# Counts of a graph kernel: a third of each row widened from SBUF by GpSimd and by a transfer, three row buffers, a lag of three

## The chip, the core and the metric

One NeuronCore of a Trainium2 chip runs the whole program in one launch. The metric is the device time of that launch in microseconds. The kernel before takes 4137.85 us (median of three runs, 4137.58 to 4137.88).

## The reference, cut to what matters

Four graph networks run one after the other on 6250 nodes of 128 features and 100000 edges. Each of their layers gathers the state of every edge's source node and adds it up at the edge's target node:

```python
for i in range(3):                                   # first network
    agg = segment_sum(h[src], dst, num_segments=6250)
    h = h + agg
    h = relu(bn(h @ W1[i] + b1[i]))
    h = relu(bn(h @ W2[i] + b2[i]))
# then: an attention layer with a GRU cell, five GRU steps over the same edges,
# and a last layer: segment_sum(h[src], dst) @ W.T + b
```

Between the networks stand a layer norm and additions. The input x is normalised row by row before the first layer, so that the first layer sums the normalised x over the edges.

## The kernel before, in words

Nodes are padded to 49 blocks of 128. The kernel never gathers by edge. It sorts the edges once, and from the sorted list it makes a matrix of counts: how many edges run from node s to node t, one byte each, 6272 rows of 6400 bytes, kept in HBM as `count`. Each layer's sum over the edges is then a product of the states with this matrix on TensorE: a block of 128 rows of bytes is read into SBUF (`ring`), widened to fp32r (`wide`), and multiplied with the states of the 128 source nodes. The states are cut in two parts, `hi` and `lo`, so that two matmuls with fp32r operands give the precision wanted. The target columns are handled in three thirds (`THIRDS`, `THIRD_PAIRS`), since PSUM holds no more than a third's sums at once.

The program has three stretches: `sort_edges` (to about 290 us), `fill_counts` (to 555 us) and then the layers, run by `Flow`, to the end. The change is in `fill_counts` alone, apart from one list of semaphores in `program` (line 2763).

**What the fill does.** For each of the 49 source blocks k it makes the 128 rows of the count matrix and stores them; beside that it already forms the sums of the middle third (`EARLY` = 1, 2048 columns) for the first layer, so that `Flow` is given that third (`given=(EARLY,)`). The engines run these programs, each written out by hand for all k and tied by semaphores:

- VectorE (L571 to 604), for each k: `apart` (an XOR of two int16 tables of 3200 columns, L579), `left` (a comparison of bf16 tables of 3200 columns, L580), `right` (a tensor_scalar on `apart`, L582), then `high` of block k - 2 (128 columns, L589) and `lo` of block k - `EARLY_LAG` (L596). It may run one block ahead of TensorE: before `apart` of block k it waits for all the matmuls of block k - 2. All inputs and outputs of these five lie in SBUF. After the last block it adds the finished sums to the state in four pieces of 512 columns (L602).
- TensorE (L607 to 639), for each k in four groups g: up to eight matmuls of 128 columns, one for each pair of column blocks, 25 in all (L621, `ps<-right,left`); with the last group a transpose of the state (L626); and behind each group two matmuls of 512 columns for the sums of block j = k - `EARLY_LAG`, with `hi` and with `lo` of block j (L634). The first of these waits for `hi`, `lo` and for the widened counts of block j.
- ScalarE (L641 to 676), for each k: the normalised state (L659), then for each group the move of the counts from PSUM to the row buffer as uint16, which is two count bytes (L667: three of 1024 columns and one of 128), with `hi` of a block (L654) behind the first and a spread of codes (L647) behind the second, and at last the transposed state (L674). Before it writes row buffer k % 2 it waits until the transfer of row k - 2 to HBM has landed.
- SyncE (L689 to 692): stores row k to `count` when its four groups are out.
- GpSimd (L678 to 686): waits until the store of row k has landed and until the slot of `wide` (four slots) is free, and then issues a transfer that reads the 2048 bytes of the middle third back from `count` in HBM and widens them to fp32r on the way into `wide` (L685). In this stretch it does nothing else.

The two row buffers lie in `net.aggT`, before and behind the columns of the middle third, which stay free until the sums are added. The stage ends when every engine is through its program; for GpSimd that means that the last store has landed.

The lines that the steps below touch most:

```python
        rows = [net.aggT[:, c0:c0 + ROW // 4].bitcast(U16) for c0 in (0, early.stop)]
        ...
                if k >= 2:
                    e.wait_ge(stored[k % 2], 16 * (k // 2))
        ...
                e.wait_ge(stored[k % 2], 16 * (k // 2 + 1))
        ...
                e.dma_start(wide[:, k % EARLY_SLOTS, :], count[k * P:(k + 1) * P, t0 * PAIR:t0 * PAIR + width])\
                    .then_inc(s[f"loaded{k % EARLY_SLOTS}"], 16)
```

Of the kernel before, what the change touches and what calls it, by code (L numbers as in the profile page):

```python
# [11 lines left out]
U8 = mybir.dt.uint8  # L12
U16 = mybir.dt.uint16
# [11 lines left out]
P = 128  # L25
NB = -(-N // P)
NP = NB * P
# [14 lines left out]
PAIR = 2 * P  # L42
NCHUNK = (NB + 1) // 2
ROW = NCHUNK * PAIR
# [13 lines left out]
THIRD_PAIRS = [(0, 10), (10, 8), (18, 7)]  # L58
# [20 lines left out]
GATE_SLOTS = 11  # L79
EARLY = 1  # L80
EARLY_BANK = 4
EARLY_LAG = 4
EARLY_CUT = 2
EARLY_SLOTS = 4
CODE_SLOTS = 4
# [443 lines left out]
def fill_counts(nc, net, count, hot, seen, stored):  # L529
# [4 lines left out]
    ps = net.ps  # L534
# [3 lines left out]
    PER = 8  # L538
    groups = -(-NCHUNK // PER)
    pieces = SUMS[EARLY]  # L540
    width = sum(size for _, size in pieces)
    codes_each = NCHUNK * RUN
    assert len(pieces) == groups == 4
    names = ["left", "apart", "right", "mm", "out", "spread", "normal", "turned", "state", "high", "hi", "lo", "summed", "whole",
             *[f"loaded{j}" for j in range(EARLY_SLOTS)]]
    with ExitStack() as tmp, stage(nc, *names, held=stored) as (block, s):
        left = [scratch(nc, tmp, f"left{u}", [P, P, NCHUNK], BF16) for u in (0, 1)]
# [4 lines left out]
        hi = scratch(nc, tmp, "hi", [P, CUT_SLOTS, P], F32R)  # L552
        lo = scratch(nc, tmp, "lo", [P, CUT_SLOTS, P], F32R)
        early = slice(THIRDS[EARLY][0] * P, sum(THIRDS[EARLY]) * P)
        rows = [net.aggT[:, c0:c0 + ROW // 4].bitcast(U16) for c0 in (0, early.stop)]
        codes_by = net.aggT[:, ROW // 4:ROW // 4 + CODE_SLOTS * codes_each // 2].bitcast(I16)
        assert early.start >= ROW // 4 + CODE_SLOTS * codes_each // 2 and early.stop + ROW // 4 <= NP and early.stop - early.start == width

        def of_block(table, k, run):
            row = table[:, k * NCHUNK * run:(k + 1) * NCHUNK * run]  # L560
# [8 lines left out]
        @block.vector  # L569
        def _(e):  # L570
            for k in range(NB + EARLY_LAG):  # L571
                u = k % 2
                if k < NB:
                    if k >= 2:
                        e.wait_ge(s["mm"], groups * (k - 1))
                    e.wait_ge(s["spread"], k + 1)
                    if k:
                        e.wait_ge(s["right"], k)
                    e.tensor_tensor(apart[:, :, :], marks_by[:, :, :], of_block(codes_by, k % CODE_SLOTS, RUN), ALU.bitwise_xor).then_inc(s["apart"], 1)  # L579
                    e.tensor_tensor(left[u][:, :, :], orders_by[:, :, :], of_block(row_of, k, 1), ALU.is_equal).then_inc(s["left"], 1)  # L580
                    e.wait_ge(s["apart"], k + 1)
                    e.tensor_scalar(flat(right[u]), apart[:, :, :], 256.0, 256.0, ALU.min, ALU.subtract).then_inc(s["right"], 1)  # L582
                j = k - EARLY_CUT
                if 0 <= j < NB:
                    e.wait_ge(s["normal"], j + 1)
                    if j >= EARLY_SLOTS:
                        e.wait_ge(s["hi"], j - EARLY_SLOTS + 1)
                        e.wait_ge(s["lo"], j - EARLY_SLOTS + 1)
                    e.tensor_scalar(high[:, j % EARLY_SLOTS, :], source(j).bitcast(I32), HIGH_BITS, None, ALU.bitwise_and)\  # L589
                        .then_inc(s["high"], 1)  # L590
                j = k - EARLY_LAG
                if j >= 0:
                    e.wait_ge(s["high"], j + 1)
                    if j >= CUT_SLOTS:
                        e.wait_ge(s["summed"], j - CUT_SLOTS + 1)
                    e.tensor_tensor(lo[:, j % CUT_SLOTS, :], source(j), high[:, j % EARLY_SLOTS, :].bitcast(F32), ALU.subtract)\  # L596
                        .then_inc(s["lo"], 1)
            e.wait_ge(s["state"], NB)
            for c, (w0, size) in enumerate(pieces):
                o = slice(early.start + w0, early.start + w0 + size)  # L600
                e.wait_ge(s["whole"], c + 1)
                e.tensor_tensor(net.aggT[:, o].rearrange("p (t u f) -> p t u f", u=2, f=P),  # L602
                                ps[:, EARLY_BANK + c, 0:size].rearrange("p (t f u) -> p t u f", u=2, f=P),
                                net.hT[:, o].rearrange("p (t u f) -> p t u f", u=2, f=P), ALU.add)

        @block.tensor
        def _(e):  # L607
            for k in range(NB + EARLY_LAG):
                u, j = k % 2, k - EARLY_LAG
                for g in range(groups):  # L610
                    bank = g % 2 * 2
                    if k < NB:
                        if g == 0:
                            e.wait_ge(s["left"], k + 1)
                            e.wait_ge(s["right"], k + 1)
                        if groups * k + g >= 2:
                            e.wait_ge(s["out"], groups * k + g - 1)
                        if g == 1 and k:
                            e.wait_ge(s["state"], k)
                        for t in range(PER * g, min(PER * g + PER, NCHUNK)):  # L620
                            ins = e.matmul(ps[:, bank + t % PER // 4, t % 4 * P:(t % 4 + 1) * P], left[u][:, :, t],  # L621
                                           right[u][:, :, t, :], start=True, stop=True)
                        ins.then_inc(s["mm"], 1)
                        if g + 1 == groups:
                            e.wait_ge(s["normal"], k + 1)
                            e.transpose(ps[:, TURN, 0:P], source(k), net.ident[:, :]).then_inc(s["turned"], 1)  # L626
                    if j >= 0:
                        w0, size = pieces[g]
                        if g == 0:
                            e.wait_ge(s["hi"], j + 1)  # L630
                            e.wait_ge(s["lo"], j + 1)
                            e.wait_ge(s[f"loaded{j % EARLY_SLOTS}"], j // EARLY_SLOTS * 16 + 16)
                        for part in (hi, lo):
                            ins = e.matmul(ps[:, EARLY_BANK + g, 0:size], part[:, j % CUT_SLOTS, :], wide[:, j % EARLY_SLOTS, w0:w0 + size],  # L634
                                           start=j == 0 and part is hi, stop=j == NB - 1 and part is lo, skip_group_check=True)
                        if j == NB - 1:
                            ins.then_inc(s["whole"], 1)
                        elif g + 1 == groups:
                            ins.then_inc(s["summed"], 1)

        @block.scalar  # L641
        def _(e):
# [15 lines left out]
            for k in range(NB):  # L658
                e.activation(source(k), net.xN[:, k * P:(k + 1) * P], ACT.Relu, scale=inv[:, k:k + 1],  # L659
                             bias=off[:, k:k + 1]).then_inc(s["normal"], 1)  # L660
                if k >= 2:
                    e.wait_ge(stored[k % 2], 16 * (k // 2))
                for g in range(groups):
                    t0, t1 = PER * g, min(PER * g + PER, NCHUNK)
                    bank = g % 2 * 2
                    e.wait_ge(s["mm"], groups * k + g + 1)
                    e.activation(rows[k % 2][:, t0 * P:t1 * P], ps[:, bank:bank + 2, :].rearrange("p b f -> p (b f)")  # L667
                                 [:, 0:(t1 - t0) * P], ACT.Copy, scale=-1.0).then_inc(s["out"], 1)
                    if g == 0 and k + 1 >= EARLY_LAG:
                        cut(k + 1 - EARLY_LAG)  # L670
                    if g == 1 and k + 2 < NB:
                        spread(k + 2)
                e.wait_ge(s["turned"], k + 1)
                e.copy(net.hT[:, k * P:(k + 1) * P], ps[:, TURN, 0:P]).then_inc(s["state"], 1)  # L674
# [2 lines left out]

        @block.gpsimd  # L678
        def _(e):
            t0 = THIRD_PAIRS[EARLY][0]  # L680
            for k in range(NB):
                e.wait_ge(stored[k % 2], 16 * (k // 2 + 1))
                if k >= EARLY_SLOTS:
                    e.wait_ge(s["summed"], k - EARLY_SLOTS + 1)
                e.dma_start(wide[:, k % EARLY_SLOTS, :], count[k * P:(k + 1) * P, t0 * PAIR:t0 * PAIR + width])\  # L685
                    .then_inc(s[f"loaded{k % EARLY_SLOTS}"], 16)

        @block.sync
        def _(e):  # L689
            for k in range(NB):  # L690
                e.wait_ge(s["out"], groups * (k + 1))
                e.dma_start(count[k * P:(k + 1) * P, :], rows[k % 2].bitcast(U8)).then_inc(stored[k % 2], 16)


def count_anything(nc, net, src, dst, count, more):
# [1944 lines left out]
def program(nc, a, out):  # L2640
# [3 lines left out]
    with ExitStack() as ctx:  # L2644
        net = Net(nc, ctx)
# [98 lines left out]
            norm_factors(ch, vec, bn)  # L2744
            norm_rows(ch)

        stored = [nc.alloc_semaphore(f"count_stored{u}_{nc.next_id()}") for u in (0, 1)]
        roots = [(bn[:, 0, :], vec[:, 4, :]), (rows_bn[:, 6, :], rows_bn[:, 4, :])]
        build_counts(nc, net, a["src"], a["dst"], count, many[:, :], (matrices, vectors, directs, a["x"]), (roots, factor_work), stored)
        early.close()  # L2750
# [86 lines left out]
```

## Time and profile before

| What | Value |
|---|---|
| median of three runs | 4137.85 us |
| the profiled execution's own time | 4137.52 us |
| its span in the trace | 4135.9 us |
| mean TensorE clock granted over the span | 0.99 |
| TensorE, VectorE, ScalarE, GpSimd busy | 91%, 74%, 60%, 33% |
| `apart` of the first and of the last block of the fill starts | 290.3 us, 529.1 us |
| first read of `count` by the layers, at the start of the next stage | 555.1 us |
| moved by DMA between 290 and 560 us | 92.89 MB, mean 344 GB/s |

All times in the trace are counted from the start of the span. The profiled execution's own time is 1.6 us above its span and 0.33 us under the median of the three runs. PE, DVE, ACT, POOL and SP are the trace's names for TensorE, VectorE, ScalarE, GpSimd and SyncE; L579 is line 579 of the kernel.

### The profile page before, as it was taken

What the parts mean: (1) busy time and instruction counts of PE and PEld (TensorE: products, weight loads), DVE (VectorE), ACT (ScalarE), POOL (GpSimd) and SP (SyncE); (2) the same over time, 40 slices, a digit from 0 to 9 for tenths busy, and PEclk for the clock granted to TensorE, in tenths of its full rate; (3) what the DMA queues carried; (4) which work ended last, traced back from release to release, by engine and by line L of the source; (5) the groups of instructions that cost most, each with busy time, mean ns of one, the idle gap of its engine ahead of it and who ended that gap; (6) DMA issues with size and microseconds to landing.
All of it is one profiled execution on the core that took longest, in us unless ns stands there. A gap on an engine that the chain in (4) does not pass through costs nothing.

```text
span 4135.9 us, 59814 instructions
## 1 busy us (share of the span) xinstructions
PE 3774.8 (91%) x17331; PEld 2948.2 (71%) x17331; DVE 3061.5 (74%) x5526; ACT 2479.4 (60%) x4705; POOL 1381.2 (33%) x2017
## 2 busy tenths in 40 slices
PE   0128889999999999999899999999999999999999
PEld 0116578888888644555588888888888888887887
DVE  9989956577677677887668767766866876786685
ACT  1118756656656787787565655565565565566655
POOL 0021135533545320000362343244244234456624
PEclk9999999999999999999899999999999999999999
DMA  2019964544543322222143344344444334433444
GB/s 63 0 52 381 364 224 125 141 130 124 144 128 107 95 69 76 70 66 56 46 114 107 107 130 120 108 125 122 111 120 122 110 104 130 119 97 108 114 133 135
DMA packets 234209, 496.24 MB, mean 120 GB/s; under 512 B 32579, under 2 KB 100924, under 8 KB 227223
## 3 DMA queue, kind: packets, MB, share of 16 engines
q1 hardware_dynamic: 213084, 432.93, 36.6%
q0 software_dynamic: 7856, 53.36, 3.6%
q10 hardware_dynamic: 12938, 6.05, 0.7%
q8 instruction: 146, 2.39, 0.3%
q14 instruction: 185, 1.52, 0.1%
HBM read 409.83 MB, written 43.87 MB: 110 GB/s over the span
## 4 chain that ended last, share of the span: by engine, by line
PE 50%; issue 0%; DVE 0%; POOL 0%; ACT 0%; ACTq 0%; POOLq 0%; DVEq 0%
PE ps L2170 40%; PE ps L2288 3%; PE ps L2289 3%; PE ps L2291 1%; PE ps L2290 1%; PE ps L2332 1%; PE ps L2313 0%; PE ps L2318 0%; PE ps L2274 0%; PE ps L2202 0%; PE ps L2208 0%; PE ps L2193 0%; ACT wide L2017 0%; PE ps L2185 0%; POOL inv L2072 0%
## 5 line engine op out<-in xcount | busy, mean ns | idle before, releaser
L2170 PE MATMUL ps<-wide,hi 128*128 128x512 f32 (+2 forms) x5537 | 2139.0, 389 | 26.2 <-issue 11.0
L2170 PE MATMUL ps<-wide,lo 128*128 128x512 f32 (+2 forms) x5537 | 2078.2, 379 | 0.0
L2017 DVE CAST wide<-ring 128x1536 fp32r<-128x1536 uint8 (+2 forms) x1274 | 1311.1, 1029 | 560.8 <-PE ps L2170 555.1
L2170 PEld LDWEIGHTS ps<-wide,hi 128*128 128x128 f32 x5537 | 1043.0, 188 | 230.8 <-issue 32.9
L2170 PEld LDWEIGHTS ps<-wide,lo 128*128 128x128 f32 x5537 | 1044.8, 189 | 186.1
L2017 ACT CAST wide<-ring 128x768 fp32r<-128x768 uint8 (+1 forms) x1274 | 1153.1, 905 | 4.3 <-DMA ring<-count 3.0
L2384 ACT CAST hi<-high 128x128 fp32r<-128x128 f32 x1274 | 381.6, 300 | 991.5 <-PE ps L2170 616.2
L2109 POOL TENSOR_TENSOR lo<-hN,high 128x128 fp32r<-128x128 f32 x686 | 567.7, 831 | 757.9 <-PE ps L2170 469.2
L2109 POOL TENSOR_TENSOR lo<-hB,high 128x128 fp32r<-128x128 f32 x588 | 497.5, 847 | 763.3 <-PE ps L2170 543.9
L2166 PE MATMUL ps<-hN,hB 128*128 128x512 f32 (+1 forms) x1274 | 525.3, 569 | 5.6 <-DVE aggT L2347 4.2
L2377 ACT ACTIVATE hN<-aggT,source_scores 128x512 f32<-128x512 f32 (+1 forms) x637 | 428.8, 695 | 118.1 <-PE ps L2166 86.9
L2513 DVE TENSOR_TENSOR hN<-hN,ring 128x512 f32<-128x512 f32 (+1 forms) x637 | 402.7, 668 | 109.2 <-ACT hN L2377 104.2
L2166 PEld LDWEIGHTS ps<-hN,hB 128*128 128x128 f32 x1274 | 241.0, 190 | 263.7 <-issue 208.9
L2538 DVE SCALAR_TENSOR_TENSOR room<-ps,b2h,room 128x256 f32<-128x256 f32 (+1 forms) x125 | 59.8, 479 | 247.8 <-ACT room L2405 247.8
L2522 DVE TENSOR_SCALAR high<-hN 128x128 int32<-128x128 int32 x686 | 235.0, 343 | 9.3 <-POOL lo L2109 3.7
L2522 DVE TENSOR_SCALAR high<-hB 128x128 int32<-128x128 int32 x588 | 204.9, 348 | 0.9 <-POOL lo L2109 0.9
L667 ACT ACTIVATE aggT<-ps 128x1024 uint16<-128x1024 f32 x196 | 159.2, 842 | 53.7 <-DMA count<-aggT 30.8
L472 PE MATMUL ps<-ident,aggT 128*128 128x128 f32 x112 | 27.6, 428 | 168.0 <-DVE aggT L182 168.0
L621 PEld LDWEIGHTS ps<-right,left 128*128 128x128 bf16 x1225 | 101.6, 158 | 106.6 <-issue 53.8
L2289 PE MATMUL ps<-hT,wT 128*128 128x256 f32 (+1 forms) x600 | 175.8, 375 | 0.0
L2405 ACT ACTIVATE room<-ps,b2s 128x256 f32<-128x256 f32 (+1 forms) x250 | 103.8, 466 | 118.2 <-PE ps L2291 117.9
L2071 POOL TENSOR_SCALAR states_bn<-states_bn 128x1 f32<-128x1 f32 x1 | 0.2, 230 | 505.5 <-POOLq L142 505.5
(247 smaller groups left out, 3498.5 us busy)
## 6 DMA issues: line engine op xcount, KB each, us to landing
ring<-count SPq DMA_DIRECT2D x490, 320.0 KB, 2.9
ring<-count SPq DMA_DIRECT2D x441, 256.0 KB, 2.6
ring<-count SPq DMA_DIRECT2D x490, 224.0 KB, 2.5
wide<-count POOLq DMA_DIRECT2D x49, 1024.0 KB, 5.7
count<-aggT SPq DMA_DIRECT2D x49, 800.0 KB, 5.1
xN<-in_x ACTq DMA_DIRECT2D x1, 2744.0 KB
out<-xN SPq DMA_DIRECT2D x1, 1064.0 KB
out<-xN SPq DMA_DIRECT2D x1, 896.0 KB
```

What stands on the lines that cost most here:

```text
L667: e.activation(rows[k % 2][:, t0 * P:t1 * P], ps[:, bank:bank + 2, :].rearrange("p b f -> p (b f)") [:, 0:(t1 - t0) * P], ACT.Copy, scale= ...
L2017: return copy(wide[:, g % WIDE_SLOTS, c0:c1].rearrange("p (t u f) -> p t u f", u=2, f=P), rows[:, g % row_slots, c0:c1].rearrange("p (t f ...
L2109: e.tensor_tensor(lo[:, g % CUT_SLOTS, :], source(n, k), high[:, g % CUT_SLOTS, :].bitcast(F32), ALU.subtract)\
L2166: ins = e.matmul(ps[:, c, 0:size], source(n, k), weights(g, c), start=k == 0, stop=k == NB - 1, skip_group_check=True)
L2170: ins = e.matmul(ps[:, c, 0:size], part[:, g % CUT_SLOTS, :], wide[:, g % WIDE_SLOTS, w0:w0 + size], start=k == 0 and part is hi, stop=k = ...
L2288: e.matmul(o, gates_of(c)[g_], net.aggT[:, c.cols], start=True, stop=False)
L2289: e.matmul(o, gru.w_state[g_], net.hT[:, c.cols], start=False, stop=True)
L2377: e.activation(weights(g, c), layers[n].target_scores[:, sums_at(q, c)], ACT.Sigmoid, bias=layers[n].source_scores[:, k:k + 1]).then_inc(s ...
L2384: e.copy(hi[:, g % CUT_SLOTS, :], high[:, g % CUT_SLOTS, :].bitcast(F32)).then_inc(s["hi"], 1)
L2405: e.activation(room[i][u][:, 0:c.size], ps[:, bank, i * PAIR:i * PAIR + c.size], ACT.Sigmoid, bias=self.step(c).b_sum[i]).then_inc(s["rz"], 1)
L2513: e.tensor_tensor(gate, gate, rows[:, g % row_slots, c0:c1].rearrange("p (t f u) -> p t u f", u=2, f=P), ALU.mult).then_inc(s["weighed"], 1)
L2522: e.tensor_scalar(high[:, g % CUT_SLOTS, :], source(n, k).bitcast(I32), HIGH_BITS, None, ALU.bitwise_and)\
```

## The change

GpSimd no longer reads the middle third back from HBM. For each block it waits until two of the four groups of the row are in the row buffer, and itself copies the first 1024 of the 2048 columns from the row buffer to `wide`, widening bytes to fp32r; then it waits for the third group and issues a transfer from the row buffer in SBUF to `wide` for the other 1024 columns, which widens on the way as before. Nothing of this waits for the store to HBM any more. There are three row buffers in place of two (the third lies in the columns of the middle third themselves), and each is written again when its store, its copy and its transfer are through. The sums run three blocks behind the fill in place of four. TensorE waits for the copied half before its first group of sums and for the transferred half before its third. VectorE waits for the stores of the third buffer and for all copies before it writes the sums over it, and SyncE waits at the end for all stores.

```diff
-EARLY_LAG = 4
+EARLY_LAG = 3
+EARLY_COPIED = 2
+ROW_BUFFERS = 3
...
-        rows = [net.aggT[:, c0:c0 + ROW // 4].bitcast(U16) for c0 in (0, early.stop)]
+        rows = [net.aggT[:, c0:c0 + ROW // 4].bitcast(U16) for c0 in (0, early.start, early.stop)]
...
             e.wait_ge(s["state"], NB)
+            e.wait_ge(stored[1], 16 * len(range(1, NB, ROW_BUFFERS)))
+            e.wait_ge(s["copied"], NB)
...
                             e.wait_ge(s["lo"], j + 1)
+                            e.wait_ge(s["copied"], j + 1)
+                        if g == EARLY_COPIED:
                             e.wait_ge(s[f"loaded{j % EARLY_SLOTS}"], j // EARLY_SLOTS * 16 + 16)
...
-                if k >= 2:
-                    e.wait_ge(stored[k % 2], 16 * (k // 2))
+                if k >= ROW_BUFFERS:
+                    j = k - ROW_BUFFERS
+                    e.wait_ge(stored[k % ROW_BUFFERS], 16 * (k // ROW_BUFFERS))
+                    e.wait_ge(s["copied"], j + 1)
+                    e.wait_ge(s[f"loaded{j % EARLY_SLOTS}"], j // EARLY_SLOTS * 16 + 16)
...
-            t0 = THIRD_PAIRS[EARLY][0]
+            c0 = THIRD_PAIRS[EARLY][0] * PAIR
+            c1, c2 = c0 + pieces[EARLY_COPIED][0], c0 + width
+            near, far = ((c - 1) // (PER * PAIR) + 1 for c in (c1, c2))
             for k in range(NB):
-                e.wait_ge(stored[k % 2], 16 * (k // 2 + 1))
+                row = rows[k % ROW_BUFFERS].bitcast(U8)
                 if k >= EARLY_SLOTS:
                     e.wait_ge(s["summed"], k - EARLY_SLOTS + 1)
-                e.dma_start(wide[:, k % EARLY_SLOTS, :], count[k * P:(k + 1) * P, t0 * PAIR:t0 * PAIR + width])\
-                    .then_inc(s[f"loaded{k % EARLY_SLOTS}"], 16)
+                e.wait_ge(s["out"], groups * k + near)
+                e.tensor_copy(wide[:, k % EARLY_SLOTS, 0:c1 - c0], row[:, c0:c1]).then_inc(s["copied"], 1)
+                e.wait_ge(s["out"], groups * k + far)
+                e.dma_start(wide[:, k % EARLY_SLOTS, c1 - c0:width], row[:, c1:c2]).then_inc(s[f"loaded{k % EARLY_SLOTS}"], 16)
...
             for k in range(NB):
                 e.wait_ge(s["out"], groups * (k + 1))
-                e.dma_start(count[k * P:(k + 1) * P, :], rows[k % 2].bitcast(U8)).then_inc(stored[k % 2], 16)
+                e.dma_start(count[k * P:(k + 1) * P, :], rows[k % ROW_BUFFERS].bitcast(U8)).then_inc(stored[k % ROW_BUFFERS], 16)
+            for u in range(ROW_BUFFERS):
+                e.wait_ge(stored[u], 16 * len(range(u, NB, ROW_BUFFERS)))
```

With `c0` = 2560, `c1` = 3584 and `c2` = 4608, `near` is 2 and `far` is 3.

## Rows read from the trace of the kernel before

**Rows 1.** The page's first line

```profile
span 4135.9 us, 59814 instructions
```

**Rows 2.** Windows: us, busy of PE, PEld, DVE, ACT, POOL, clock, DMA, GB/s

```profile
350.00:400.00 50.00, 44.12 (x363) 31.28 (x362) 50.00 (x52) 42.24 (x83) 7.19 (x11) 1.00 1.08 401
...
421.00:424.40 3.40, 3.40 (x19) 2.36 (x19) 1.65 (x3) 2.89 (x6) 0.72 (x2) 0.50 0.83 306
```

**Rows 3.** Timeline of VectorE, one block: start us, us, line, operation

```profile
401.82 1.82 DVE L579 TENSOR_TENSOR apart<-marks_by,aggT 128x3200 int16<-128x3200 int16 x1
403.56 1.89 DVE L580 TENSOR_TENSOR left<-orders_by,row_of 128x3200 bf16<-128x3200 bf16 x1
405.36 0.99 DVE L582 TENSOR_SCALAR right<-apart 128x3200 bf16<-128x3200 int16 x1
...
406.60 1.82 DVE L579 TENSOR_TENSOR apart<-marks_by,aggT 128x3200 int16<-128x3200 int16 x1
```

**Rows 4.** Line 579: min/median/max ns, first and last start; its idle time, times

```profile
L579 DVE TENSOR_TENSOR apart<-marks_by,aggT x49: 1810/1821/1827, 290.3 to 529.1; 128x3200 int16<-128x3200 int16 x49
...
  PE ps L621: 8.7, 12
```

**Rows 5.** Waits from 310 to 540 us: total us, times, longest

```profile
ACT aggT L667 <- DMA count<-aggT: 30.8, 17, 2.8
```

**Rows 6.** Timeline of ScalarE and TensorE in the same block

```profile
403.60 1.03 ACT L667 ACTIVATE aggT<-ps 128x1024 uint16<-128x1024 f32 x1
...
405.45 0.40 PE L634 MATMUL ps<-wide,lo 128*128 128x512 f32 x1
406.45 0.72 PE L621 MATMUL ps<-right,left 128*128 128x128 bf16 x8 [0.61 <-DVE right L582]
```

**Rows 7.** Timeline of GpSimd and VectorE in a layer, GpSimd beside two casts

```profile
2177.64 1.24 POOL L2109 TENSOR_TENSOR lo<-hN,high 128x128 fp32r<-128x128 f32 x1 [0.94 <-PE ps L2170]
2179.82 0.46 POOL L2109 TENSOR_TENSOR lo<-hN,high 128x128 fp32r<-128x128 f32 x1 [0.94 <-PE ps L2170]
...
2177.60 0.96 DVE L2017 CAST wide<-ring 128x1536 fp32r<-128x1536 uint8 x1 [0.81 <-PE ps L2170]
2178.48 0.49 DVE L2522 TENSOR_SCALAR high<-hN 128x128 int32<-128x128 int32 x1
2179.78 1.49 DVE L2017 CAST wide<-ring 128x1280 fp32r<-128x1280 uint8 x1 [0.81 <-PE ps L2170]
2181.19 0.22 DVE L2522 TENSOR_SCALAR high<-hN 128x128 int32<-128x128 int32 x1
```

**Rows 8.** Timeline: GpSimd, then VectorE with two SBUF inputs

```profile
2309.66 0.97 POOL L2109 TENSOR_TENSOR lo<-hN,high 128x128 fp32r<-128x128 f32 x1 [0.48 <-PE ps L2170]
...
2310.23 0.68 DVE L2546 TENSOR_TENSOR hT<-hT,room 128x256 f32<-128x256 f32 x1
2310.95 0.42 DVE L2547 TENSOR_TENSOR hT<-hT,room 128x256 f32<-128x256 f32 x1
```

**Rows 9.** Timeline of GpSimd at the start, VectorE not against it

```profile
1.11 0.29 POOL L421 TENSOR_SCALAR_AFFINE_SELECT ident<-ident 128x128 f32<-128x128 f32 x1
1.36 0.53 POOL L423 MEMSET zero<- 128x512 bf16 x1
...
2.24 1.20 POOL L428 IOTA number_row<- 128x1280 int32 x1
```

**Rows 10.** Timeline of the fill's end

```profile
552.40 0.39 PE L634 MATMUL ps<-wide,hi 128*128 128x512 f32 x1
...
552.63 0.39 PE L634 MATMUL ps<-wide,lo 128*128 128x512 f32 x1
555.10 6.37 SPq L2054 DMA_DIRECT2D ring<-count  x11
```

**Rows 11.** Line 685, GpSimd's transfers into wide: us to landing

```profile
DMA to landing us min/median/max: 4.6/5.7/8.1
```

**Rows 12.** Line 692, the stores to HBM

```profile
DMA to landing us min/median/max: 3.3/5.1/7.6
```

More of the change, by code:

```diff
@@ L543, in fill_counts @@
     assert len(pieces) == groups == 4
-    names = ["left", "apart", "right", "mm", "out", "spread", "normal", "turned", "state", "high", "hi", "lo", "summed", "whole",
+    names = ["left", "apart", "right", "mm", "out", "spread", "normal", "turned", "state", "high", "hi", "lo", "summed", "whole", "copied",
              *[f"loaded{j}" for j in range(EARLY_SLOTS)]]
@@ L554, in fill_counts @@
         early = slice(THIRDS[EARLY][0] * P, sum(THIRDS[EARLY]) * P)
-        rows = [net.aggT[:, c0:c0 + ROW // 4].bitcast(U16) for c0 in (0, early.stop)]
+        rows = [net.aggT[:, c0:c0 + ROW // 4].bitcast(U16) for c0 in (0, early.start, early.stop)]
+        assert len(rows) == len(stored) == ROW_BUFFERS
         codes_by = net.aggT[:, ROW // 4:ROW // 4 + CODE_SLOTS * codes_each // 2].bitcast(I16)
-        assert early.start >= ROW // 4 + CODE_SLOTS * codes_each // 2 and early.stop + ROW // 4 <= NP and early.stop - early.start == width
+        assert early.start >= ROW // 4 + CODE_SLOTS * codes_each // 2 and early.stop + ROW // 4 <= NP and early.stop - early.start == width >= ROW // 4
         def of_block(table, k, run):
@@ L666, in _ @@
                     e.wait_ge(s["mm"], groups * k + g + 1)
-                    e.activation(rows[k % 2][:, t0 * P:t1 * P], ps[:, bank:bank + 2, :].rearrange("p b f -> p (b f)")
+                    e.activation(rows[k % ROW_BUFFERS][:, t0 * P:t1 * P], ps[:, bank:bank + 2, :].rearrange("p b f -> p (b f)")
                                  [:, 0:(t1 - t0) * P], ACT.Copy, scale=-1.0).then_inc(s["out"], 1)
@@ L2745, in factor_work @@
             norm_rows(ch)
-        stored = [nc.alloc_semaphore(f"count_stored{u}_{nc.next_id()}") for u in (0, 1)]
+        stored = [nc.alloc_semaphore(f"count_stored{u}_{nc.next_id()}") for u in range(ROW_BUFFERS)]
         roots = [(bn[:, 0, :], vec[:, 4, :]), (rows_bn[:, 6, :], rows_bn[:, 4, :])]
```

## The prediction, made before the changed kernel ran

> **What bounds the kernel now.** I read first where the changed stage lies and who is never idle in it. The span is 4135.9 us [rows 1]; the profiled execution's own time is 4137.52 us, 0.33 under the median of 4137.85. Everything changed lies in the fill, from about 290 to 555 us. The windows [rows 2] show its steady state: in 50 us VectorE is busy for 50.00, ScalarE for 42.24, TensorE for 44.12 and GpSimd for 7.19, at full TensorE clock. So VectorE sets the pace. Its timeline [rows 3] shows one block: `apart` starts at 401.82 and again at 406.60, a period of 4.78 us, with `left`, `right`, `high` and `lo` back to back between. TensorE by contrast waits in each block for `right` (0.61 us idle before 406.45, [rows 6]).
>
> The stage doesn't quite keep that period: from the first `apart` to the last are 529.1 - 290.3 = 238.8 us [rows 4] for 48 periods, which at 4.78 would be 229.4. The 9.4 us above are nearly VectorE's 8.7 us of idle time in 12 waits for TensorE's counts [rows 4], and behind these stands ScalarE, which waited 17 times, 30.8 us in all, for a store to land before it could write a row buffer again [rows 5].
>
> After the last `apart` (529.1) the next stage starts only at 555.10 [rows 10], 26.0 us later: the last store must land, then the read back must land (5.7 us median, [rows 11]), then four blocks of sums follow.
>
> **What it removes.** (1) The store waits. A buffer now has three periods in place of two, over 14 us, for a store that lands in 5.1 us and never took over 7.6 [rows 12]; and the DMA load falls, since 1024 of 2048 widened columns come by no transfer and none is read from HBM. I take the whole 9.4 us; at least nothing. (2) The tail. A block's matmuls start at 406.45, 4.63 us after its `apart` (401.82), and take 4.78 - 0.61 = 4.17 us, so they end 8.8 us after it [rows 3, 6]. Behind the last block three blocks of sums remain, 3 x 8 matmuls at 0.23 us (552.40 to 552.63), 5.5 us. From the end of the sums (552.63 + 0.39) to the next stage were 2.1 us [rows 10]. Together 8.8 + 5.5 + 2.1 = 16.4 us in place of 26.0: 9.6 us gained. The last transfer into `wide` is issued about when TensorE ends block 48 and is needed at the last set's third piece, 2 x 1.84 + 0.92 = 4.6 us later; the present one, twice as large, lands in 4.6 at best and 5.7 in the median [rows 11]. So it may cost 1 us, which I leave to the range, and the last store (5.1 us, [rows 12]) lands before the sums end.
>
> **What it adds: a copy on GpSimd beside a saturated VectorE.** GpSimd works in the fill only as an issuer of transfers now, so its own time is free. The question is whether its reads and writes of SBUF hold VectorE. A layer's timeline shows it [rows 7]: a GpSimd operation that takes 0.46 us when it runs beside the cast of 1280 columns takes 1.24 us beside that of 1536. It starts at 2177.64, the cast ends at 2178.56, and GpSimd ends at 2178.88: it waited for the cast. VectorE's next operation, `high`, then takes 0.49 us in place of 0.22: it waited for GpSimd. The same holds for an operation with two inputs in SBUF, the form of `apart` and `left`: L2546 takes 0.68 us behind a waiting GpSimd operation (2309.66), and L2547, of the same shape, 0.42 [rows 8]. So a GpSimd operation that arrives while VectorE works gets in at the next boundary, and delays VectorE by its own length less about 0.19 us (0.46 alone, 0.27 and 0.26 lost).
>
> Where does the copy arrive? ScalarE ends the second group of a row at 403.60 + 1.03 = 404.63 [rows 6], inside `left` of the next block (403.56 to 405.45, [rows 3]). The copy gets in behind it and pushes `right`, which TensorE waits for. This happens once in each period: blocks 0 to 47, 48 times. The copy of block 48 finds VectorE done.
>
> How long is the copy? The trace before has none. GpSimd's memset of 512 columns took 0.53 us and its iota of 1280 took 1.20 [rows 9], 0.87 ns a column, which gives 0.53 + 512 x 0.87 ns = 0.98 us for 1024; neither reads SBUF. The nearest that reads one input, a select of 128 columns, took 0.29 [rows 9]; eight of them, 2.35 us, are the bound above, since their fixed part is counted eight times. Below, the copy may hold nothing. I take 1.0 us, since a copy has one input, as the select has, and no arithmetic; the hold is then 1.0 - 0.19 = 0.81 us, and 48 x 0.81 = 38.9 us. The ends for the range are 0 and 48 x 2.16 = 104 us.
>
> The Trainium skill (GPSIMD Engine Reference, section 3.1) says that a tight loop on GpSimd takes 1.8 cycles an element at best, 769 ns for 512 elements; no row here shows that. As an estimate from it the copy would take 1.54 us and hold 1.35, and the sum below would come to 4183 us.
>
> **The other edits.** The third buffer costs nothing by itself. The waits that ScalarE gets for the copy and the transfer of row k - 3 are for work more than two periods old, as is TensorE's for row k - 3. If `wide` came late, TensorE would stand before its sums and with it the groups of counts queued behind; the margin is about two periods, over 9 us. `hi` and `lo` of block k - 3 keep their places beside work of the same period. GpSimd's issue of the transfer is there already and VectorE's durations in the fill are constant beside it (1810 to 1827 ns for `apart`, [rows 4]), so it goes on at nothing; the transfer is queued behind the copy, and who waits for it is TensorE three blocks on. SyncE's stores are queued behind nothing new, and its waits at the end lie beside the sums.
>
> **The sum.** 38.9 - 9.4 - 9.6 = 19.9 us slower: 4137.5 + 19.9 = 4157.4 against the profiled execution, 4158 against the median. The period becomes 4.78 + 0.81 = 5.6 us.
>
> **Rivals.** A: the copy doesn't hold VectorE, because it slips in where VectorE doesn't use what they share, or takes turns with it. For it: VectorE's times in the fill are constant beside GpSimd's transfer issues. Against: [rows 7, 8]. Then only the gains remain, 19.0 us: 4118.5. The two sides part at a hold of 19.0 / 48 = 0.40 us, a copy of 0.59 us, that is at 0.6 ns a column, faster than any row.
> B: the copy is longer, as far as 2.35 us. With 1.5 us of hold it is 72 - 19 = 53 us slower, 4190.5; at the bound 104 - 19, 4222. For it: GpSimd's operations that read are dearer a column than those that only write (0.29 us for 128 columns).
> C: TensorE's clock. With a period of 5.6 us TensorE idles 1.4 us in each block, and the chip did grant half the clock in the fill once it had idled: in the window 421.00:424.40 TensorE ran at 0.50 and took 3.40 / 19 = 0.18 us a matmul, against 44.12 / 363 = 0.12 at full clock [rows 2]. A block has 34 matmuls, 6.1 us at half clock, more than 5.6. If the clock stayed low, TensorE would be the bound and it would cost 0.5 x 48 = 24 us more, 4182. A single low stretch costs almost nothing, since VectorE has slack behind it.
> D: the relief isn't one, and ScalarE still waits for stores: 9.4 us more, 4167; at a period of 5.6 us and three buffers that is unlikely.
>
> **Chances.** Forecast, with D in it: 0.50. B and C: 0.24. A: 0.20. A hold near the break-even: 0.06. The predicted time is the forecast's, 4158. The range goes from A, 4117, to B with 1.5 us of hold, 4190; the far end of B stays out. Without A, the forecast's own range is 4145 to 4175. A measurement here can tell 0.2%, 8.3 us, from no change; within that lie holds of 0.22 to 0.57 us. So faster 0.22, same 0.06, slower 0.72.
>
> **What would show it.** `apart` should start every 5.6 us, with `right` at about 1.8 us in place of 0.99 in nearly every block, and a GpSimd copy that starts inside `left` and lasts until after `left` ends. ScalarE's wait for stores should be near nothing, and from the last `apart` to the next stage there should be 17 us. I am wrong if `right` stays at 0.99, or if the copy is shorter than 0.6 us once it has begun, and in size if the copy's own part is well over 1 us.

## The result, and the profile after

The changed kernel takes 4165.38 us (median of four runs, 4163.73 to 4167.53) against 4137.72 beside it: a ratio of 1.0068, 95% interval 1.005 to 1.0085, or 27.7 us slower. Forecast was slower, 4158 in a range of 4117 to 4190.

The page's first line and the windows of the changed kernel (columns as in [rows 2]):

```profile
span 4163.4 us, 59911 instructions
```

```profile
350.00:400.00 50.00, 37.38 (x306) 26.50 (x306) 50.00 (x46) 35.61 (x71) 22.18 (x19) 1.00 0.67 243
```

VectorE is still busy for all of the 50 us, but it does 46 operations there in place of 52 [rows 2], and TensorE and ScalarE do less with it. TensorE's clock is full, and the DMA share is 0.67 in place of 1.08. So VectorE is still the bound and has become slower. Its timeline, with GpSimd's beside it, shows where (start us, us, line, operation; compare [rows 3, 6]):

```profile
401.73 1.81 DVE L582 TENSOR_TENSOR apart<-marks_by,aggT 128x3200 int16<-128x3200 int16 x1
403.47 1.88 DVE L583 TENSOR_TENSOR left<-orders_by,row_of 128x3200 bf16<-128x3200 bf16 x1
405.27 1.82 DVE L585 TENSOR_SCALAR right<-apart 128x3200 bf16<-128x3200 int16 x1
...
407.35 1.81 DVE L582 TENSOR_TENSOR apart<-marks_by,aggT 128x3200 int16<-128x3200 int16 x1
```

```profile
404.68 1.57 POOL L698 CAST wide<-aggT 128x1024 fp32r<-128x1024 uint8 x1 [3.09 <-ACT aggT L677]
406.19 1.02 POOL L700 DMA_DIRECT2D wide<-aggT  x1
```

The copy (a CAST in the trace) starts at 404.68, inside `left`, waits for the end of `left` at 405.35 and runs until 406.25. `right` takes 1.82 us in place of 0.99, and `apart` starts again after 5.62 us in place of 4.78. TensorE then waits 1.46 us for `right` in each block, in place of 0.61:

```profile
407.19 0.72 PE L626 MATMUL ps<-right,left 128*128 128x128 bf16 x8 [1.46 <-DVE right L585]
```

The bounds of the fill (line 582 is what line 579 was), the copy of block 48, when VectorE had nothing left to do, the next stage's start, and the issues between 300 and 570 us with their sizes and median us to landing:

```profile
L582 DVE TENSOR_TENSOR apart<-marks_by,aggT x49: 1809/1811/1829, 296.1 to 564.7; 128x3200 int16<-128x3200 int16 x49
```

```profile
573.22 1.05 POOL L698 CAST wide<-aggT 128x1024 fp32r<-128x1024 uint8 x1 [3.09 <-ACT aggT L677]
```

```profile
582.27 15.95 SPq L2070 DMA_DIRECT2D ring<-count  x15
```

```profile
count<-aggT SPq DMA_DIRECT2D x48, 800.0 KB, 3.3
wide<-aggT POOLq DMA_DIRECT2D x48, 512.0 KB, 4.5
```

Read against [rows 4] and [rows 10], the 27.2 us at the start of the next stage (582.27 - 555.10) split so:

| Stretch | before | after | difference |
|---|---|---|---|
| up to the first `apart` | 290.3 | 296.05 | +5.8 |
| from the first to the last `apart` | 238.8 | 268.6 | +29.8 |
| from the last `apart` to the next stage | 26.0 | 17.6 | -8.4 |

The second and the third are what the prediction described. The first is new: it lies ahead of the fill. Below, the stretch from the first to the last `apart` is called the fill, the one from there to the next stage the tail, and the time from one `apart` to the next the period.

### The profile page after: what moved, and what is told of

The parts are those of the page before. It is cut to its first block, busy times and chain, and to the rows that moved or that the text cites. A ratio compares the mean times of both kernels' runs of the same rounds, so it can differ in the third digit from the quotient of the medians.

```text
span 4163.4 us, 59911 instructions
## 1 busy us (share of the span) xinstructions
PE 3767.6 (90%) x17331; PEld 2944.6 (71%) x17331; DVE 3099.5 (74%) x5526; ACT 2477.3 (60%) x4705; POOL 1468.7 (35%) x2066
## 4 chain that ended last, share of the span: by engine, by line
PE 50%; issue 0%; POOL 0%; ACT 0%; DVE 0%; ACTq 0%; POOLq 0%
PE ps L2186 40%; PE ps L2304 3%; PE ps L2305 3%; PE ps L2306 1%; PE ps L2307 1%; PE ps L2348 1%; PE ps L2329 0%; PE ps L2334 0%; PE ps L2290 0%; PE ps L2218 0%; PE ps L2224 0%; PE ps L2209 0%; ACT wide L2033 0%; PE ps L2201 0%; POOL inv L2088 0%
## 5 line engine op out<-in xcount | busy, mean ns | idle before, releaser
L2186 PE MATMUL ps<-wide,hi 128*128 128x512 f32 (+2 forms) x5537 | 2139.6, 389 | 25.2 <-issue 10.3
L2186 PEld LDWEIGHTS ps<-wide,hi 128*128 128x128 f32 x5537 | 1043.4, 188 | 229.6 <-issue 31.7
L626 PE MATMUL ps<-right,left 128*128 128x128 bf16 x1225 | 125.7, 244 | 77.6 <-DVE right L585 76.7
```

The source lines that it names most:

```text
L2186: ins = e.matmul(ps[:, c, 0:size], part[:, g % CUT_SLOTS, :], wide[:, g % WIDE_SLOTS, w0:w0 + size], start=k == 0 and part is hi, stop=k = ...
```

## The experiments

The theory: GpSimd's copy waits for the VectorE operation it meets, gets in behind it, and holds the next one for its own length. Rivals: the transfer between two places of SBUF or the shorter lag lengthens the period; the hold is a fixed price; TensorE's wait, not VectorE's lost time, is what costs. Open were the late start and the size of the gains. In each group of runs (1 to 4, 5 to 8, 9 to 11, and 12) the kernel before ran on the same chip.

| Run | median us | ratio to before (95%) | fill, us | tail, us |
|---|---|---|---|---|
| the changed kernel again | 4158.51 | 1.0066 (1.005 to 1.0083) | 268.5 | 17.6 |
| before, one semaphore more | 4130.67 | 1.0 (0.999 to 1.001) | 232.3 | 23.3 |
| all by transfer | 4120.75 | 0.9977 (0.9967 to 0.9987) | 229.0 | 19.4 |
| copy of 512 | 4137.93 | 1.0019 (1.0009 to 1.0029) | 248.4 | 18.4 |
| memset in place of the copy | 4129.60 | 0.9996 (0.9987 to 1.0005) | 241.2 | 17.0 |
| copy for the last block alone | 4117.48 | 0.9968 (0.9956 to 0.998) | 229.2 | 17.3 |
| copy later | 4159.54 | 1.0068 (1.0053 to 1.0083) | 275.1 | 17.5 |
| copy on VectorE | 4146.79 | 1.004 (1.0025 to 1.0056) | 257.8 | 17.2 |
| before, again | 4130.16 | 1.0003 (0.9993 to 1.0012) | 233.2 | 23.3 |
| the changed kernel, a third time | 4157.82 | 1.0067 (1.0046 to 1.0089) | 268.5 | 17.6 |
| three buffers alone | 4124.46 | 0.9987 (0.9977 to 0.9996) | 229.6 | 23.1 |
| copy later, again (one run) | 4166.62 | no interval; 4132.6 beside it, one run | 268.3 | 20.3 |

The kernel before took 4130.1, 4130.7 and 4129.9 us (medians) beside the first three groups, 7 to 8 us less than on the first chip.

**1. The changed kernel again.** No edit.

> The changed kernel, unchanged, to see what of its time recurs. Theory (the copy holds VectorE once in a period): the 48 periods of the fill take 268.6 us again, 5.62 each. Open: the first apart started 5.8 us later than before, with VectorE waiting about 1 us for its own semaphore in several steps of the sort stage. If that belongs to the program (it has one more semaphore allocated ahead of the sort), the first apart starts near 296 again; rival: it is chance of one execution, and the first apart starts near 290 and the time is about 4160.

The periods came out the same to 0.1 us. The late start didn't:

```profile
L582 DVE TENSOR_TENSOR apart<-marks_by,aggT x49: 1809/1812/1827, 291.0 to 559.5; 128x3200 int16<-128x3200 int16 x49
```

Yet the ratio is the same as on the first chip, so the late start alone doesn't explain why the loss is 28 and not 20 us. Experiments 2 and 9 bear on that.

**2. One semaphore more.**

```diff
-        stored = [nc.alloc_semaphore(f"count_stored{u}_{nc.next_id()}") for u in (0, 1)]
+        stored = [nc.alloc_semaphore(f"count_stored{u}_{nc.next_id()}") for u in (0, 1, 2)]
```

> The kernel before with one more semaphore allocated ahead of the sort and not used. If the number of the semaphore that VectorE counts with decides the late start of the fill, this is slower than before by about 5.8 us (4143.5) with the first apart near 296. Rival: the delay comes with other parts of the changed program or by chance, and this stays at 4137.7 with the first apart near 290.

The first `apart` started at 290.6 us, and the time is that of before (4130.67 and 4130.12). But the changed kernel had no late start on this chip either (experiment 1), so this run can't rule the semaphore out where the late start does appear.

**3. All by transfer.** GpSimd's copy goes, and with it every wait for `copied`; TensorE waits for the transfer before its first group of sums (only GpSimd's lines are shown):

```diff
-                e.wait_ge(s["out"], groups * k + near)
-                e.tensor_copy(wide[:, k % EARLY_SLOTS, 0:c1 - c0], row[:, c0:c1]).then_inc(s["copied"], 1)
                 e.wait_ge(s["out"], groups * k + far)
-                e.dma_start(wide[:, k % EARLY_SLOTS, c1 - c0:width], row[:, c1:c2]).then_inc(s[f"loaded{k % EARLY_SLOTS}"], 16)
+                e.dma_start(wide[:, k % EARLY_SLOTS, 0:width], row[:, c0:c2]).then_inc(s[f"loaded{k % EARLY_SLOTS}"], 16)
```

> The changed kernel without GpSimd's copy: the transfer from the row buffer in SBUF widens all 2048 columns. Theory (the copy holds VectorE by 0.84 us in each of 48 periods): right is back at 0.99 us, the period at 4.78, and the time falls by about 40 us against the changed kernel, to 4125 with the late start and 4119 without it. Rival (the period grew for another reason, the transfer between two places of SBUF or the shorter lag): the period stays above 5.2 us and the time near 4165.

`right` is back, and with it the fill; the second and third row bound fill and tail:

```profile
L585 DVE TENSOR_SCALAR right<-apart x49: 973/974/992, 294.0 to 523.0; 128x3200 bf16<-128x3200 int16 x49
...
L582 DVE TENSOR_TENSOR apart<-marks_by,aggT x49: 1804/1807/1828, 290.5 to 519.5; 128x3200 int16<-128x3200 int16 x49
...
538.88 19.57 SPq L2064 DMA_DIRECT2D ring<-count  x17
```

The fill takes 229.0 us, 39.5 less, and the median is 37.8 us under the changed kernel's on the same chip (4158.51 - 4120.75). The whole loss is GpSimd's copy; the transfer, the lag and the buffers have no part in it. What is left of the change is 9.4 us faster than before beside it (4130.12). The DMA share is high again (1.03 in the window from 350 to 400 us), the full-width transfer lands in 6.6 us, and TensorE waits for it at the end, which experiment 6 takes up:

```profile
534.74 0.47 PE L638 MATMUL ps<-wide,hi 128*128 128x512 f32 x1 [2.29 <-DMA wide<-aggT]
```

**4. A copy of 512 columns.**

```diff
-EARLY_COPIED = 2
+EARLY_COPIED = 1
```

> The changed kernel with a copy of 512 columns in place of 1024, the transfer taking the other 1536. Theory (VectorE is held for the length of the copy less some 0.2 us): a copy of 0.58 us, a hold of 0.38, a period of 5.16 us and a time 22 us under the changed kernel's, 4143. Rival (the hold is a fixed price of having any GpSimd operation in between): the period stays at 5.6 us and the time at 4165.

```profile
L585 DVE TENSOR_SCALAR right<-apart x49: 987/1398/1405, 293.6 to 542.1; 128x3200 bf16<-128x3200 int16 x49
```

```profile
541.47 1.14 POOL L698 CAST wide<-aggT 128x512 fp32r<-128x512 uint8 x1 [3.09 <-ACT aggT L677]
...
546.66 0.62 POOL L698 CAST wide<-aggT 128x512 fp32r<-128x512 uint8 x1 [3.09 <-ACT aggT L677]
```

The copy takes 0.62 us where VectorE is done (the second row), and `right` 1.40 us, 0.41 us more than before; the period is 5.19 us, against 5.16 expected. The time is 20.6 us under the changed kernel's on the same chip, against 22. With 1024 columns it was 1.05 us alone and 0.84 of hold. So the hold is the copy's length less 0.21 us in both, and copy and hold both grow by 0.84 ns a column. The rival's fixed price falls.

**5. A memset in place of the copy.** This kernel leaves out the sums of the copied half; they are zero.

```diff
-                e.tensor_copy(wide[:, k % EARLY_SLOTS, 0:c1 - c0], row[:, c0:c1]).then_inc(s["copied"], 1)
+                e.memset(wide[:, k % EARLY_SLOTS, 0:c1 - c0].bitcast(F32), 0.0).then_inc(s["copied"], 1)
```

> The changed kernel with a memset to zero of the same 1024 columns of wide in place of GpSimd's copy: GpSimd writes as much but reads nothing (the sums of the copied half are left out, they come out as zero). Theory in two forms. If what the two engines share is used by any GpSimd operation on SBUF, the memset waits for the end of left too and right is held: period about 5.6 us. If left (two inputs, no fast mode with a second write) shares only its second read, the memset runs beside left from its start at out of the second group, 0.8 us before left ends, and only its last 0.1 to 0.2 us holds right: period 4.8 to 5.0 us and a time some 30 to 38 us under the changed kernel's.

```profile
454.13 0.95 POOL L698 MEMSET wide<- 128x1024 f32 x1 [3.08 <-ACT aggT L677]
```

```profile
452.92 1.88 DVE L583 TENSOR_TENSOR left<-orders_by,row_of 128x3200 bf16<-128x3200 bf16 x1
454.73 1.21 DVE L585 TENSOR_SCALAR right<-apart 128x3200 bf16<-128x3200 int16 x1
```

The memset starts inside `left` like the copy, but it doesn't wait: it takes 0.95 us, until 455.08. Only what of it lies behind the end of `left` (454.80) holds `right`, by 0.22 us. So `left`, with two inputs in SBUF, keeps GpSimd from reading and not from writing, while `right`, with one input, is kept back by a GpSimd operation that only writes. The first half is the rule of the Trainium skill (SBUF — State Buffer, Who interferes with whom) that a VectorE operation with two SBUF inputs contends with a GpSimd operation that reads SBUF, and not with one that only writes it; the trace agrees. The period was 5.00 us, the upper end of what was expected; the time is 28.9 us under experiment 1's, on another chip, and 30 to 38 were expected.

**6. A copy for the last block alone.** Experiment 3, with the copy kept for block 48 (only GpSimd's lines are shown; TensorE waits for this copy before the first sums of block 48, and for the transfer before the third):

```diff
+                cut = c0
+                if k == NB - 1:
+                    cut = c1
+                    e.wait_ge(s["out"], groups * k + near)
+                    e.tensor_copy(wide[:, k % EARLY_SLOTS, 0:c1 - c0], row[:, c0:c1]).then_inc(s["copied"], 1)
                 e.wait_ge(s["out"], groups * k + far)
-                e.dma_start(wide[:, k % EARLY_SLOTS, 0:width], row[:, c0:c2]).then_inc(s[f"loaded{k % EARLY_SLOTS}"], 16)
+                e.dma_start(wide[:, k % EARLY_SLOTS, cut - c0:width], row[:, cut:c2]).then_inc(s[f"loaded{k % EARLY_SLOTS}"], 16)
```

> All 2048 columns by transfer as in the run before, but for the last block, whose first 1024 columns GpSimd copies: VectorE has nothing left to hold there, and the last transfer is half as large. Theory: period 4.78 us as there, and from the last apart to the next stage 17.6 us as in the changed kernel less the hold of 0.84, so 16.8, against 19.4 with all by transfer: 2.6 us less than that run, about 12 us under the kernel before. Rival: the last transfer isn't what ends last, and it stays at 19.4.

```profile
L582 DVE TENSOR_TENSOR apart<-marks_by,aggT x49: 1807/1811/1825, 289.9 to 519.1; 128x3200 int16<-128x3200 int16 x49
...
536.48 21.90 SPq L2073 DMA_DIRECT2D ring<-count  x18
```

From the last `apart` to the next stage it is 17.3 us in place of 19.4, 0.5 more than expected, and 4117.48 is the fastest of all, 13.2 us under the kernel before beside it (4130.73). The copy is of use where VectorE is idle. Against experiment 3 the gain shows in the tails of the two traces; the medians come from different chips.

**7. The copy later.**

```diff
-                e.wait_ge(s["out"], groups * k + near)
+                e.wait_ge(s["out"], groups * k + far)
                 e.tensor_copy(wide[:, k % EARLY_SLOTS, 0:c1 - c0], row[:, c0:c1]).then_inc(s["copied"], 1)
```

> The changed kernel with its copy issued after the third group of a row in place of the second, so that it comes while VectorE is in right and gets in before high. Theory (a saturated VectorE loses the copy's length wherever it comes): right is 0.99 us again, one of high, lo or apart is longer by 0.84, and the period stays at 5.62 us, the time within 3 us of the changed kernel's. Rival (the price is TensorE's wait for right, so that a copy that holds another operation is cheap): period under 5.2 us and 20 us or more less.

```profile
451.45 0.98 DVE L585 TENSOR_SCALAR right<-apart 128x3200 bf16<-128x3200 int16 x1
452.36 1.06 DVE L592 TENSOR_SCALAR high<-hN 128x128 int32<-128x128 int32 x1
```

`right` is short again and `high` pays in its place, 1.06 us for 0.22. The period stays at 5.62 us. It isn't TensorE's wait for `right` that costs: VectorE is full, and it loses 0.84 us at whichever operation comes behind the copy. (In two periods, from 340.24 us on, the copy met `apart`, and `left` took 2.73 and 2.72 us for 1.88.) The fill took 275.1 us and not 268.5 because of one copy:

```profile
316.66 15.23 POOL L698 CAST wide<-aggT 128x1024 fp32r<-128x1024 uint8 x1 [4.59 <-ACT aggT L677]
331.83 0.53 POOL L700 DMA_DIRECT2D wide<-aggT  x1
332.35 1.05 POOL L698 CAST wide<-aggT 128x1024 fp32r<-128x1024 uint8 x1
```

```profile
DVE apart L582 <- PE ps L626: 9.3, 1, 9.3
```

While this copy waited, 14 operations of VectorE ended and the next one began each time, in three periods of 4.78 us. It got in only when VectorE had stopped (its last operation started at 330.70), since ScalarE waited for the transfer queued behind the copy, and TensorE for ScalarE; VectorE then waited 9.3 us for TensorE (from the waits between 325 and 350 us).

**8. The copy on VectorE.** The same 1024 columns, issued on VectorE behind `left` of the next block, and no copy on GpSimd:

```diff
                     e.tensor_tensor(left[u][:, :, :], orders_by[:, :, :], of_block(row_of, k, 1), ALU.is_equal).then_inc(s["left"], 1)
+                    if k:
+                        widen(e, k - 1)
```

> The changed kernel with the copy of the 1024 columns issued on VectorE itself, behind left of the next block, and none on GpSimd. Theory: VectorE loses what it takes to do the copy, 0.69 us a cast of 1024 columns in the layers, of which some 0.08 overlaps with its neighbours: a period of 4.78 + 0.61 = 5.39 us, 48 x 0.23 = 11 us under the changed kernel's time. Rival (GpSimd's engine time is worth having, the hold is only partly VectorE's): on VectorE it is no cheaper, period 5.6 us or more.

```profile
454.50 0.68 DVE L580 CAST wide<-aggT 128x1024 fp32r<-128x1024 uint8 x1
455.10 0.97 DVE L599 TENSOR_SCALAR right<-apart 128x3200 bf16<-128x3200 int16 x1
```

The cast costs VectorE 0.60 us (454.50 to 455.10) and the period is 5.38 us; the time is 13 us under experiment 7's on the same chip. So help from GpSimd costs VectorE more (0.84 us) than doing the work itself.

**9. The kernel before, again.** No edit.

> The kernel before, to see how far its fill and tail vary between executions. Theory: its stalls behind the stores are a matter of when they land, so that the profile the prediction rests on (9.4 us over 48 clean periods, 26.0 us from the last apart to the next stage) is one draw; a profile here shows between 2 and 10 us of stall and 23 to 26 us of tail. Rival: both are fixed and come out the same again.

```profile
L579 DVE TENSOR_TENSOR apart<-marks_by,aggT x49: 1805/1817/1827, 290.3 to 523.5; 128x3200 int16<-128x3200 int16 x49
```

```profile
ACT aggT L667 <- DMA count<-aggT: 12.8, 8, 2.6
```

ScalarE waits 12.8 us for stores in place of 30.8 [rows 5] (310 to 545 us). The fill takes 233.2 us and the tail 23.3, together 8.4 us less than in [rows 4, 10], and the span is 7.9 us shorter (4135.9 - 4128.0); the medians differ by as much (4137.7 and 4130.1). The profile the prediction rests on had more of the stalls that the change removes than this one has. One of them lies in its tail, behind the last `apart`:

```profile
532.50 1.02 ACT L667 ACTIVATE aggT<-ps 128x1024 uint16<-128x1024 f32 x1 [2.81 <-DMA count<-aggT]
```

TensorE began block 48 7.6 us after the last `apart` there and 4.6 us here, where ScalarE had no such wait; that is about the difference of the two tails, 2.7 us.

**10. The changed kernel, a third time.** No edit.

> The changed kernel once more. Theory: period 5.62 us and fill 268.5 us again. If the late start of the fill (296.05 in place of 290.3, from VectorE's waits for its own semaphore around 276 to 283 us) is chance, the first apart starts within 1 us of 290.5; if it belongs to the changed program on some chips it may be seen here again.

The period was 5.62 us, the fill 268.5 us, and the first `apart` at 290.2. Against experiment 9, on the same chip, the fill is 35.3 us longer and the tail 5.7 shorter, 29.6 us together; the spans, 4156.3 and 4128.0, differ by 28.3.

**11. Three buffers alone.** The kernel before, with every `% 2` of the row buffers made `% 3` and the third buffer of the change:

```diff
-                if k >= 2:
-                    e.wait_ge(stored[k % 2], 16 * (k // 2))
+                if k >= ROW_BUFFERS:
+                    e.wait_ge(stored[k % ROW_BUFFERS], 16 * (k // ROW_BUFFERS))
```

> The kernel before with three row buffers and nothing else changed: the read back from HBM, the lag of four and the DMA load stay. Theory (with a third buffer no store is late): ScalarE's waits for stores are gone, the fill takes 229.3 us, and the tail is that of the kernel before, 23 to 26 us: 3 to 9 us faster than before. Rival (the DMA queues are too loaded for a third buffer to help, and wide arrives late in its place): TensorE waits for wide, and the time is that of the kernel before within 2 us.

```profile
L580 DVE TENSOR_TENSOR apart<-marks_by,aggT x49: 1806/1809/1827, 291.2 to 520.8; 128x3200 int16<-128x3200 int16 x49
```

Here ScalarE's waits for stores are gone and the fill takes 229.6 us, as expected, with the tail unchanged at 23.1. It is 5.5 us faster than before and its runs lie closer together (4123.65 to 4125.60) than those of before beside them (4123.73 to 4137.14): the third buffer by itself takes the stall away.

**12. The later copy once more.** The kernel of experiment 7. The expectation calls the long copy that of the seventh block; it was the fourth copy, of block 3, and 15 operations of VectorE ended in that time, at the last of which it got in.

> The kernel with the later copy once more. In its first profile one copy, of the seventh block, lasted 15.23 us: it got in neither at the end of one VectorE operation nor of the next twelve, until VectorE itself stood idle. If the later place makes this happen, some copy lasts over 5 us again and the fill is well over 269 us; if it was chance, the longest copy lasts under 3 us and the fill takes 268.5 to 270 us. The period is 5.62 us in either case.

The longest copy took 2.32 us, so the long one didn't come again. But the late start did: the first `apart` started at 294.9. The tail, 20.3 us, was longer than in experiment 7 because of the last transfer:

```profile
579.45 0.79 PE L641 MATMUL ps<-wide,hi 128*128 128x512 f32 x1 [2.30 <-DMA wide<-aggT]
```

It took 5.8 us to landing, where that of experiment 7 took 3.8 and TensorE waited 0.27 us for it; and the four matmuls behind the wait began 0.43 to 0.59 us apart in place of 0.23 (the granted clock was 0.50 from 580 to 584 us). The two single runs differ by 34.0 us (4166.62 - 4132.6), 6 more than the changed kernel's 28; the late start, 4.6, and the longer tail, 2.7, account for it roughly.

## Why the prediction was right, and what it missed

**The hold on VectorE was right in mechanism, place and size.** The copy arrives inside `left`, waits for its end and pushes `right`, once in each period. It was priced at 1.0 us with a hold of 0.81; measured are 1.05 us where nothing is in its way, and 0.84. The period was forecast as 5.6 us and is 5.62. The price per column, 0.87 ns from GpSimd operations that read nothing [rows 9], was 0.84. That a copy, which reads, would cost no more than they do was argued and stood in no row; it came out so. The bound from the select was far too long. So would have been the estimate of 1.54 us by the Trainium skill (GPSIMD Engine Reference, section 3.1), which took the section's 1.8 cycles an element. The same section puts short loop bodies (k ≤ 2) at 1.03 cycles, at 1.2 GHz an estimate of 0.86 ns; the 0.84 ns of experiment 4 agree with that.

**The store waits.** They went altogether, as forecast. The row for them [rows 5] was one execution's: 9.4 us there, and 3.8 in experiment 9 (233.2 - 229.4). This term was mis-sized for the other chips, since the sum took one profile's stall for the kernel's. Whether the chip or the execution sets the stall is open: the kernel before kept within 1.2 us on the first chip and spread over 13 us on the others. The prediction also says that TensorE waits in each block for `right`; in that profile it did so in 16 of 49 blocks, and this carries none of the terms.

**The tail** was forecast as 16.4 us without the hold and came to 17.6 with the 0.84 of the last hold in it, so 16.8. But before it was 23.3 us on the other chips in place of 26.0; the 26.0 had a wait for a store in it (experiment 9). The 1 us that the prediction left to the range for the last transfer showed once, as 2.3 us in experiment 12. So the two gains, summed to 19.0 us, were 3.8 + 6.5 = 10.3 there. Then 48 x 0.84 = 40.3 less 10.3 is 30 us, against some 28 measured. That the changed kernel took 4158.5 us there, the very number of the forecast, is luck: the forecast adds 20 us to 4138, and there it was 28 on 4130.

**On the first chip** the gains were there as forecast (238.8 + 26.0 before), and fill and tail alone came to 21.4 us, against 19.9. The other 5.8 us are the late start, which no step of the prediction had. The equal ratios on two chips thus have different makings. Whether all four runs on the first chip started late can't be seen; only one was profiled.

**The rivals.** A (no hold) falls with the first rows of the profile after; what it would have given, 4118.5, is near what the version without the copy took (4120.75), but that is 9.4 us under the kernel before beside it and not the 19.0 of A. B (a longer copy) falls. C (TensorE's clock) falls: at a period of 5.62 us, with TensorE idle for 1.4 us in each, the clock stayed at 1.00 from 350 to 500 us. A low stretch cost nothing, as the prediction said: in experiment 10 the mean clock was 0.86 from 300 to 350 us, and the fill took 268.5 us all the same. D (stores still late) falls.

## What to carry to other kernels

An idle GpSimd beside a saturated VectorE is not free help. Before moving a copy there, look in the trace for a GpSimd operation that reads SBUF and is longer than when it runs alone, and for the VectorE operation behind it; price the move at the GpSimd operation's own length less 0.2 us for each time (what the two copy widths here gave), and compare with what VectorE itself would take (0.84 against 0.60 us here). Such a copy pays where VectorE is idle, as in the last block, and the transfer, which GpSimd only issues, was the better way in the rest; a stall that hangs on when transfers land wants more than one profile before it is booked as a gain.

## What the runs showed that had not been expected

**A GpSimd copy can be kept out for much longer than one operation.** In the 245 copies of 1024 columns in five profiles the longest but one took 2.49 us; that one took 15.23 us, and was passed over at 14 ends of VectorE operations. The prediction's rule, that such an operation gets in at the next boundary, thus failed once. Why is open.

**VectorE can wait about a microsecond for its own semaphore.** In the first profile of the changed kernel a stretch of dependent operations of 128 columns, each of which waits for the one before, ran with gaps, while GpSimd issued indirect transfers:

```profile
275.03 0.29 DVE L986 TENSOR_TENSOR rows_bn<-rows_bn 128x128 f32<-128x128 f32 x1
276.38 0.29 DVE L987 SCALAR_TENSOR_TENSOR rows_bn<-rows_bn 128x128 f32<-128x128 f32 x1 [1.06 <-DVE rows_bn L986]
277.08 0.23 DVE L988 TENSOR_SCALAR rows_bn<-rows_bn 128x128 f32<-128x128 f32 x1 [0.41 <-DVE rows_bn L987]
278.47 0.29 DVE L989 TENSOR_TENSOR rows_bn<-rows_bn 128x128 f32<-128x128 f32 x1 [1.17 <-DVE rows_bn L988]
```

They make up the late start: L2739, the last of these operations, starts at 283.37 us here and at 277.52 in experiment 10. Of the fourteen profiles two show such gaps, this one and that of experiment 12, both of kernels that have the change; in the twelve others, three of them of the same two programs, the same operations follow each other within 0.1 us. What brings the gaps is open.
